# A transformer row kernel: V's channels stored by groups, V projected ahead of the scores in the first batch row, experts' biases added after the second gathering

## What is computed

```python
# attention block, on h = layernorm(layernorm(x)) with gains: 16 heads of 16 channels, each token sees 15 neighbours
q, k, v = split(h @ qkv_w + qkv_b)
attn = softmax(q . k[window] / 4);  h = (attn @ v[window]) @ proj_w + proj_b
x1 = layernorm(x) + h
x = x + x1 + gelu(layernorm(x1) @ fc1_w + fc1_b) @ fc2_w + fc2_b
# feed-forward block, on z = layernorm(x)
main = gelu(z @ W1m + b1m) @ W2m + b2m
top2 of softmax(mean(z) @ w_gate + b_gate)           # 2 of 8 experts for each batch row
expert_out = sum_k gate_k * (gelu(z @ W1e[k] + b1e[k]) @ W2e[k] + b2e[k])
out = x + a * main + (1 - a) * expert_out
```

## Time and profile before

| | |
|---|---|
| median of 3 runs | 1964.24 us |
| the profiled execution | 1966.04 us |
| its span, first to last instruction | 1964.3 us |
| TensorE's mean granted clock | 0.996 of full |
| DMA packets, under 512 B | 237054, 113564 |
| busy: VectorE, ScalarE, GpSimd | 70%, 61%, 44% of the span |

### The profile page before, as it was taken

One profiled execution on the slowest core, in us unless ns is written; L12 is line 12 of the kernel. 1 busy time (PEld: TensorE's weight loads), 2 busy tenths in 40 slices (PEclk: granted clock), 3 DMA queues, 4 the chain that ended last, 5 costly groups with the idle time before them and its releaser, 6 DMA issues.

```text
span 1964.3 us, 57553 instructions
## 1 busy us (share of the span) xinstructions
PE 1920.3 (98%) x23694; PEld 1727.4 (88%) x23694; DVE 1373.6 (70%) x2271; ACT 1191.2 (61%) x1863; POOL 854.6 (44%) x781
## 2 busy tenths in 40 slices
PE   5999999999999999999999999999999999999999
PEld 5788889898898988989888998988989889898898
DVE  6586776867768577686867768677685866768643
ACT  4575565756657566575655657566575665756554
POOL 4436245261543625335362452615336252452625
PEclk8999999999999999999999999999999999999999
DMA  4131130312204131131311303122031311313121
GB/s 118 57 82 55 38 83 28 93 55 54 72 23 98 50 81 56 33 88 39 92 55 37 84 28 92 55 60 72 28 93 44 87 51 34 87 39 93 44 60 54
DMA packets 237054, 122.41 MB, mean 62 GB/s; under 512 B 113564, under 2 KB 235768, under 8 KB 236792
## 3 DMA queue, kind: packets, MB, share of 16 engines
q1 hardware_dynamic: 234708, 117.57, 22.7%
q10 hardware_dynamic: 2084, 1.16, 0.2%
HBM read 85.52 MB, written 8.39 MB: 48 GB/s over the span
## 4 chain that ended last, share of the span: by engine, by line
PE 79%; DVE 12%; issue 4%; ACT 3%; POOL 1%; SPq 1%; DMA 0%; DVEq 0%; ACTq 0%; POOLq 0%
PE psB L233 45%; PE psA L233 27%; DVE hr_lo L533 3%; PE psA L1101 2%; PE psA L977 2%; PE psA L1064 2%; PE psA L1076 2%; DVE pr L607 2%; DVE pr L598 1%; DVE smax L605 1%; DVE acc L700 1%; DVE tm L693 1%; ACT qm L851 1%; ACT hr_hi L824 1%; DVE smax L612 1%
## 5 line engine op out<-in xcount | busy, mean ns | idle before, releaser
L533 DVE TENSOR_TENSOR hr_lo<-hf,hr_hi 128x512 fp32r<-128x512 f32 x512 | 476.6, 932 | 488.9 <-ACT hr_hi L824 487.7
L439 POOL TENSOR_SCALAR wx_hi<-raw 128x512 fp32r<-128x512 f32 x256 | 195.7, 764 | 727.2 <-DMA raw<-in_L_ffn_W2e 447.4
L824 ACT ACTIVATE hr_hi<-hf 128x512 fp32r<-128x512 f32 x512 | 323.9, 633 | 279.5 <-PE psB L233 191.2
L441 POOL TENSOR_TENSOR wx_lo<-raw,wx_hi 128x512 fp32r<-128x512 f32 x256 | 391.0, 1527 | 21.4
L233 PE MATMUL psB<-wx_hi,hr_hi 128*128 128x256 f32 x1024 | 288.5, 282 | 12.9 <-DVE acc L549 12.7
L233 PE MATMUL psB<-wx_hi,hr_lo 128*128 128x256 f32 x1024 | 286.3, 280 | 0.0
L233 PE MATMUL psB<-wx_lo,hr_hi 128*128 128x256 f32 x1024 | 285.8, 279 | 0.0
L820 ACT ACTIVATE hf<-psB,b1x 128x512 f32<-128x512 f32 x256 | 175.2, 684 | 174.1 <-PE psB L233 173.6
L233 PEld LDWEIGHTS psB<-wx_hi,hr_hi 128*128 128x128 f32 x1024 | 192.5, 188 | 28.0 <-issue 18.7
L233 PE MATMUL psB<-z_hi,wx_hi 128*128 128x512 f32 x512 | 212.0, 414 | 0.0
L233 PE MATMUL psB<-z_hi,wx_lo 128*128 128x512 f32 x512 | 202.5, 395 | 0.0
(11 more groups left out here) (151 smaller groups left out, 4772.6 us busy)
## 6 DMA issues: line engine op xcount, KB each, us to landing
raw<-in_L_ffn_W1e SPq DMA_DIRECT2D x256, 128.0 KB, 2.3
raw<-in_L_ffn_W2e SPq DMA_DIRECT2D x256, 128.0 KB, 2.2
vb<-vs SPq DMA_DIRECT2D x64, 192.0 KB
vb<-vs SPq DMA_DIRECT2D x62, 160.0 KB
out_x<-acc SPq DMA_DIRECT2D x32, 256.0 KB, 2.2
xin<-in_L_attn_x SPq DMA_DIRECT2D x15, 512.0 KB, 3.7
tm<-in_L_ffn_b2e SPq DMA_DIRECT2D x32, 128.0 KB, 3.0
raw<-in_L_attn_fc_w SPq DMA_DIRECT2D x8, 256.0 KB, 5.3
```

Source lines behind the costliest of these rows:

```text
L439: g.tensor_scalar(wx[0][:, s, :], raw[:, s, :], 1.0, 0.0, ALU.mult, ALU.add).then_inc(w_hi.sem, 1)
L441: g.tensor_tensor(wx[1][:, s, :], raw[:, s, :], wx[0][:, s, :].bitcast(f32), ALU.subtract).then_inc(w_lo.sem, 1)
L533: v.tensor_tensor(hr[1][:, c % 2, :], hf[:, c % 3, :], hr[0][:, c % 2, :].bitcast(f32), ALU.subtract).then_inc(h_lo.sem, 1)
L824: a.activation(hr[0][:, c % 2, :], hf[:, c % 3, :], ACT.Copy).then_inc(h_hi.sem, 1)
```

## The change

`vs` is stored by channel groups, [128, 2 groups, 4 tiles, 2 parities, 128 channels]. `values` on TensorE reads the weights' columns and writes PSUM in the order of the groups, and `values` on VectorE makes four operations of 128 elements a partition for two of 256. The bias of V is loaded in that order, by two DMAs. A copy to `vb` now moves 3 or 4 KB in one run per partition. Of `vb` only what no copy writes, and `attend` reads, is set to zero, with four small memsets.

In iteration 0 both halves of V are projected and evacuated before the scores (the second through bank 1 of `psB`).

The experts' biases are summed at step 11 into `b2sum`, which lies in `kT` (free between the last scores and the next keys), and added to `acc` at step 18, after the second gathering (`add_bias`). The first gathering reads `sx` and writes `acc`. `shortcut`, which overwrites `sx`, waits for the first gathering; ScalarE's `keys` wait for `acc_b`.

```diff
@@ -92,7 +92,7 @@
-        vs = sb("vs", [P, NT, 2, D])
+        vs = sb("vs", [P, G, NT, 2, KD * GW])
@@ -136,6 +136,7 @@
+        b2sum = kT[:, LEFT:LEFT + D]
@@ -184,28 +185,29 @@
-        small_in, rows_in = signal("small_in", 8, 16), signal("rows_in", 7, 16)
+        small_in, rows_in = signal("small_in", 8, 16), signal("rows_in", 8, 16)
...
+        consts, zeroed, dzero = signal("consts"), signal("zeroed", 2 * G), signal("dzero")
...
+        acc_s, acc_b = signal("acc", 6), signal("acc_b")
...
+        val, vs_s, vb_in = signal("val", 2), signal("vs", 8), signal("vb_in", 12, 16)
@@ -265,8 +267,8 @@
-                    src = vs[at:at + n, tiles[0] - back:tiles[-1] + 1 - back, :, :].rearrange("p i e (c g n) -> p i e c g n", c=KD, g=G)[:, :, :, :, gr, :]
-                    eng.dma_start(dst.rearrange("p i e c n -> p (i e c) n"), src.rearrange("p i e c n -> p (i e c) n")).then_inc(vb_in.sem, 16)
+                    src = vs[at:at + n, gr, tiles[0] - back:tiles[-1] + 1 - back, :, :]
+                    eng.dma_start(dst.rearrange("p i e c n -> p (i e c n)"), src.rearrange("p i e n -> p (i e n)")).then_inc(vb_in.sem, 16)
@@ -290,7 +292,10 @@
-            loads = [(dst[:, :], row(src).to_broadcast([P, D])) for src, dst in ((qkv_b[2 * D:3 * D], bv), (proj_b, bproj), (fc2_b, bfc2))]
+            loads = [(dst[:, :], row(src).to_broadcast([P, D])) for src, dst in ((proj_b, bproj), (fc2_b, bfc2))]
+            for g in range(G):
+                loads.append((bv[:, g * KD * GW:(g + 1) * KD * GW].rearrange("p (c n) -> p c n", c=KD),
+                              qkv_b[2 * D:3 * D].rearrange("(o c g n) -> o c g n", o=1, c=KD, g=G)[:, :, g, :].to_broadcast([P, KD, GW])))
@@ -306,7 +311,7 @@
-            sp.wait_ge(zeroed.sem, 1)
+            sp.wait_ge(zeroed.sem, zeroed.all(0))
@@ -448,12 +453,18 @@
-                    g.wait_ge(acc0.sem, acc0.at(t - 1))
+                    g.wait_ge(acc_s.sem, acc_s.at(t - 1, 1))
...
-            g.memset(vb[:, :, :, :, :, :], 0.0).then_inc(zeroed.sem, 1)
...
+            for gr in range(G):
+                first, n = GW * gr, zeroed.per // G * gr
+                g.memset(vb[first:first + LEFT, 0, 0, :, :, :], 0.0).then_inc(zeroed.sem, 1)
+                g.wait_ge(zeroed.sem, n + 1)
+                g.memset(vb[first:first + KW, HS - 1, NT - 1, :, :, :], 0.0).then_inc(zeroed.sem, 1)
+                g.wait_ge(zeroed.sem, n + 2)
@@ -490,7 +501,7 @@
-            zeros = [kT[:, 0:LEFT], kT[:, LEFT + T:ZW], pr[:, 1, :, :, KW:].rearrange("p b g k -> p (b g) k"), vs[:, :, :, :].rearrange("p i e n -> p (i e n)")]
+            zeros = [kT[:, 0:LEFT], kT[:, LEFT + T:ZW], pr[:, 1, :, :, KW:].rearrange("p b g k -> p (b g) k"), vs[:, :, :, :, :].rearrange("p g i e n -> p (g i e n)")]
@@ -541,12 +552,16 @@
                         v.wait_ge(gate_s.sem, gate_s.all(f))
-                    if part:
-                        v.wait_ge(acc_s.sem, acc_s.at(f, 2 * (part - 1) + h))
+                    if part == 2:
+                        v.wait_ge(acc_b.sem, acc_b.at(f))
+                    elif part:
+                        v.wait_ge(acc_s.sem, acc_s.at(f, h))
                     else:
-                        v.wait_ge(acc0.sem, acc0.at(f))
-                    sl = acc[:, 2 * h:2 * h + 2, :].rearrange("p i n -> p (i n)")
-                    v.scalar_tensor_tensor(sl, psB[:, 2 + h, :], gates[:, part - 1:part] if part else al[:, 1:2], sl, ALU.mult, ALU.add).then_inc(acc_s.sem, 1)
+                        v.wait_ge(x2.sem, x2.at(f, h))
+                        if f:
+                            v.wait_ge(store.sem, store.at(f - 1, h))
+                    sl, old = (a[:, 2 * h:2 * h + 2, :].rearrange("p i n -> p (i n)") for a in (acc, acc if part else sx))
+                    v.scalar_tensor_tensor(sl, psB[:, 2 + h, :], gates[:, part - 1:part] if part else al[:, 1:2], old, ALU.mult, ALU.add).then_inc(acc_s.sem, 1)
@@ -580,11 +595,13 @@
+                bank = psA[:, 2 if n or t == 0 else 0, :] if t or n == 0 else psB[:, 1, :]
...
-                    dst, src, bias = (a.rearrange("p i (h e d) -> p i h e d", e=2, d=HD)[:, :, :, p, :] for a in (
-                        vs[:, 2 * n:2 * n + 2, p, :], psA[:, 2 if n or t == 0 else 0, :].rearrange("p (i n) -> p i n", n=D),
-                        bv[:, :].unsqueeze(1).to_broadcast([P, 2, D])))
-                    v.tensor_tensor(dst, src, bias, ALU.add).then_inc(vs_s.sem, 1)
+                    for g in range(G):
+                        dst, src, bias = (a.rearrange("p i (h e d) -> p i h e d", e=2, d=HD)[:, :, :, p, :] for a in (
+                            vs[:, g, 2 * n:2 * n + 2, p, :], bank.rearrange("p (i g n) -> p i g n", i=2, g=G)[:, :, g, :],
+                            bv[:, g * KD * GW:(g + 1) * KD * GW].unsqueeze(1).to_broadcast([P, 2, KD * GW])))
+                        v.tensor_tensor(dst, src, bias, ALU.add).then_inc(vs_s.sem, 1)
@@ -690,14 +707,16 @@
                 v.wait_ge(gate_s.sem, gate_s.all(f))
-                v.scalar_tensor_tensor(b2x[:, 0, :], b2x[:, 0, :], gates[:, 0:1], b2main[:, :], ALU.mult, ALU.add).then_inc(b2_s.sem, 1)
+                if f + 1 < ROWS:
+                    v.wait_ge(score.sem, score.all(f + 1))
+                v.scalar_tensor_tensor(b2sum, b2x[:, 0, :], gates[:, 0:1], b2main[:, :], ALU.mult, ALU.add).then_inc(b2_s.sem, 1)
                 v.wait_ge(b2_s.sem, b2_s.at(f, 0))
-                v.scalar_tensor_tensor(b2x[:, 0, :], b2x[:, 1, :], gates[:, 1:2], b2x[:, 0, :], ALU.mult, ALU.add).then_inc(b2_s.sem, 1)
+                v.scalar_tensor_tensor(b2sum, b2x[:, 1, :], gates[:, 1:2], b2sum, ALU.mult, ALU.add).then_inc(b2_s.sem, 1)
...
+            def add_bias(f):
                 v.wait_ge(b2_s.sem, b2_s.all(f))
-                v.wait_ge(x2.sem, x2.all(f))
-                if f:
-                    v.wait_ge(store.sem, store.all(f - 1))
-                v.tensor_tensor(acc[:, :, :], sx[:, :, :], b2x[:, 0, :].unsqueeze(1).to_broadcast([P, NT, D]), ALU.add).then_inc(acc0.sem, 1)
+                v.wait_ge(acc_s.sem, acc_s.at(f, 3))
+                v.tensor_tensor(acc[:, :, :], acc[:, :, :], b2sum.unsqueeze(1).to_broadcast([P, NT, D]), ALU.add).then_inc(acc_b.sem, 1)
@@ -708,6 +727,7 @@
+            values(0, 1)
@@ -735,12 +755,13 @@
                             shift(t, 0)
-                            values(t, 1)
+                            if t:
+                                values(t, 1)
...
                         shift(t, 1)
-                    elif q == 6 and f >= 0:
-                        route_bias(f)
+                    elif q == 18 and f >= 0:
+                        add_bias(f)
@@ -757,6 +778,8 @@
                         attended_low(t, 0)
+                    elif q == 11 and f >= 0:
+                        route_bias(f)
@@ -837,6 +860,8 @@
+                    if t > 1:
+                        a.wait_ge(acc_b.sem, acc_b.at(t - 2))
@@ -910,7 +935,7 @@
-                            a.wait_ge(zeroed.sem, 1)
+                            a.wait_ge(zeroed.sem, zeroed.all(0))
@@ -1032,12 +1057,12 @@
-                bank = 2 if n or t == 0 else 0
+                bank = psA[:, 2 if n or t == 0 else 0, :] if t or n == 0 else psB[:, 1, :]
...
-                        last = three(pe, psA[:, bank, j * D:(j + 1) * D], [z[:, k, to:to + P] for z in zT], [w[:, k, 2 * D:] for w in wqkv],
-                                     k == 0, k == KD - 1)
+                        last = three(pe, bank[:, j * D:(j + 1) * D].rearrange("p (g c n) -> p g c n", g=G, c=KD), [z[:, k, to:to + P] for z in zT],
+                                     [w[:, k, 2 * D:].rearrange("p (c g n) -> p g c n", c=KD, g=G) for w in wqkv], k == 0, k == KD - 1)
@@ -1045,7 +1070,7 @@
-                    pe.wait_ge(vs_s.sem, vs_s.at(t, 1))
+                    pe.wait_ge(vs_s.sem, vs_s.at(t, 3))
@@ -1153,9 +1179,7 @@
                             pe.wait_ge(z3_lo.sem, z3_lo.at(t - 1, 0))
-                        else:
-                            pe.wait_ge(vs_s.sem, vs_s.at(0, 1))
-                        values(t, 1)
+                            values(t, 1)
```

More of the change, by code:

```diff
@@ L191, in build @@
         xload, store = signal("xload", 1, 16), signal("store", 2, 16)
-        consts, zeroed, dzero = signal("consts"), signal("zeroed"), signal("dzero")
+        consts, zeroed, dzero = signal("consts"), signal("zeroed", 2 * G), signal("dzero")
         small_ps, small_t = signal("small_ps"), signal("small_t")
@@ L201, in build @@
         w_hi, w_lo = signal("w_hi", NX), signal("w_lo", NX)
-        acc_s, acc0 = signal("acc", 6), signal("acc0")
+        acc_s, acc_b = signal("acc", 6), signal("acc_b")
         nb_s = signal("nb")
@@ L213, in build @@
         qk, kT_s, qm_even, qm_odd = signal("qk", 4), signal("kT", KD), signal("qm_even", 8), signal("qm_odd", 8)
-        val, vs_s, vb_in = signal("val", 2), signal("vs", 4), signal("vb_in", 12, 16)
+        val, vs_s, vb_in = signal("val", 2), signal("vs", 8), signal("vb_in", 12, 16)
```

## The result

The changed kernel takes **1953.0 us** (median of 5 runs; 1952.5 to 1954.3). The kernel before, run beside it, takes 1964.2 (5 runs, 1961.6 to 1965.3). The ratio is 0.9945 (0.9931 to 0.9960). So it is faster, by 11 us where 26.8 were forecast, and 3 us above the upper end of the range.

The account below looks back on a forecast made before the run. TensorE, busy 98%, was taken as the bound, losing time to `acc` waits and V's copies. Gain 16.3 - 1.0 + 8.4 + 3.1 = 26.8 us from 1964.2, so median 1937.4 us, range 1932 to 1950.

Parts of the forecast that it names:

- The `acc` stall: TensorE's wait at chunk 8's down product, batch rows 1 to 15: 1.09 us each, 16.3 us won by moving the bias.
- I cost these at nothing: Waits added by the moved bias operations at q=11, q=18 and `shortcut`: no cost; at most 2.2 us a row without cover.
- The bias and the groups as one sum: Steady rows: 16.3 us gained by the bias part; groups lose 1.0 us, their faster copies worth nothing more to TensorE.
- miss `h_low` of chunk 7 altogether: Steady rows: sooner copies bring weight splits 5 to 8 us sooner, so GpSimd's `bproj` addition avoids VectorE's `h_low`.
- the stall stays: Rival: GpSimd's addition still starts at 261.6, the gathering stays late, only batch row 0 gains: 1953.7 us; chance 0.11.
- V's products and evacuations: V's projection: products still start 0.12 us apart, four evacuations take about 0.88 us; 1.0 us booked lost for the run.
- The rival with the strided operand: V's 384 products slow down on strided reads; at double time 46 us lost, 1983 us; chance of slower 0.06.
- The copies: V's window copies in batch row 0: about 0.5 us each to issue, 1.5 MB at 300 GB/s landed by 30.
- four copies no longer hold up the exponential: ACT in batch row 0: its four copies stop delaying the exponential for 5.7 us, making ACT 1.2 us earlier.
- Batch row 0: First row: `attend` starts at 32.4, 8.4 us sooner, plus 3.1 us from a clock that stays full.
- TensorE doesn't stand idle from 33.1, so the clock shouldn't fall: Batch row 0, 41 to 48 us: clock at 1.00 instead of 0.50, worth 3.1 us, bounds 0 and 6.2.

Follow-up runs that it names:

- the run with the copy in it: Changed kernel with the exponential of unit 3 replaced by a copy on ScalarE from batch row 1 on: 1947.0 us, ratio 0.9914.
- the split held: Changed kernel with GpSimd's weight split of chunk 13 held until the row's fourth normalisation (unit 3) is done: 1950.3 us, ratio 0.9934.
- The run with ten more idle products: Changed kernel with `attended_high(t, 0)` behind chunk 9's gelu, plus ten idle TensorE products around the first two attends in row 0: 1948.1 us.
- copies moved, the clock at 1.00 and products cut: Kernel with `attended_high` later, ScalarE's copies first and ten more idle products, then ten instead of sixteen idle products behind the second `attend`: 1947.8 us.
- the weight loads held: Changed kernel with SP's MLP weight loads from piece 8 on held in row 0 until the first `attend` is done: 1953.5 us, ratio 0.9952.
- the copies issued first: Changed kernel with `attended_high(t, 0)` behind chunk 9's gelu, and ScalarE's four window copies ahead of both exponentials in row 0: 1947.4 us.
- two kernels with equal pitch: Changed kernel with `attended_high(t, 0)` behind chunk 9's gelu, 1950.4 us, and changed kernel with unit 3's exponential replaced by a copy, 1947.0 us.
- the run with six products inside the first: Kernel with `attended_high` later, copies first and ten more idle products, but six idle products mid first `attend` replacing three before it: 1947.8 us.

## Why the prediction was off

**The `acc` stall: right in place and price, wrong in what follows.** It was 1.09 us a row with the hidden part, and it is gone. A row without any stall takes 118.04 us, and the run with the copy in it has a rest of 1873.9 us, 14.7 under the kernel before, where 15.3 were booked. What failed is the sentence "I cost these at nothing". I had looked at the waits that the change adds, and not at the next place in the row where TensorE meets VectorE. That place stands in the trace before the change, one chunk further on:

```profile
276.43 0.96 DVE L616 TENSOR_TENSOR pr<-pr,rinv 128x768 f32<-128x768 f32 x1
...
278.48 1.08 PE L1076 MATMUL psA<-ident,pr 128*112 128x128 f32 x8
```

The normalisation ended at 277.39 and `turn` followed at 278.48: 1.09 us of slack, in a row whose stall cost 1.46 and 0.24 us. So some 0.6 us of that row was bound to come back. Done for all 15 rows (slack 0.63 to 1.19 us), this gives about 2.5 us in seven rows; in the other eight the slack was larger than the stall. The new wait costs more: 0.47 us in each of twelve rows (118.51 less 118.04) and 1.1 in one, **6.8 us** in all, an estimate from these rows. What the slack before doesn't show is the collision: `turn`'s normalisation took 0.96 us in all 15 rows before, and 1.31 (or 1.30) in 14 of 15 after. In the fifteenth, and in two rows with the groups alone, it took 0.96, and no wait is listed; with the split held the waits went in all rows but one, and the pitch is 118.16, so that the collision is 0.35 of the 0.47. The last row's wait of 0.57 adds to it.

**The bias and the groups as one sum: right only because one was booked at nothing.** The prediction put the steady gain on the bias part and nothing on the groups in steady rows. The runs show either alone to be enough. The clause that GpSimd's addition can "miss `h_low` of chunk 7 altogether" was right, and it is the mechanism of the groups part there: `h_low` takes 0.68 us with the groups alone and 0.69 in the changed kernel, instead of 2.88. The rival "the stall stays" gave 1953.7, very near the time, but its mechanism is refuted: no wait for `acc` is left.

**V's products and evacuations: right.** The products start 0.12 us apart with the strided operand, four evacuations take 0.88 us. The rival with the strided operand is refuted, and the 1.0 us booked can't be told from nothing: 118.04 is what the prediction had left for a row.

**The copies: the rate nearly right, the issue mis-sized.** 268 GB/s at full share in a steady row, for 300 taken and 175 before. The Trainium skill ("DMA: Bandwidth & Descriptors", section "Why small descriptors are slow (HBM only)") says that SBUF to SBUF copies don't suffer from small pieces; here 268 against 175 GB/s speaks against it, and the measurement decides. But issuing took 0.86 us each on SP and 1.26 on ACT in row 0, where I had 0.5 (0.74, median, in steady rows, 0.87 before). That ACT's "four copies no longer hold up the exponential" failed: ScalarE stood 4.3 us before it, 2.2 of them after its input was there. And the twelve had not landed by 30 but at about 34.4, beside SP's weight loads. The count of runs is off too, without effect: 6016 runs become 384, not 376.

**Batch row 0: 11.5 us booked, 4.8 came.** `attend` started at 34.53 instead of 32.4, put down to ACT as forecast; that is 6.3 of the 8.4. The pause of 2.26 us behind it was not in the forecast in any form. The step "TensorE doesn't stand idle from 33.1, so the clock shouldn't fall" failed: TensorE stood idle from 33.7 to 34.5 and from 35.3 to 37.6, and the clock read 0.50 from 38 to 48, so the 3.1 us for 41 to 48 didn't come. The run with ten more idle products, where that stretch is at 1.00, has a row 0 shorter by 1.5, half of the term. With copies moved, the clock at 1.00 and products cut, VectorE's normalisations hold TensorE up, and row 0 ends at 67.21: 8.5 of the 11.5.

**The sum of the misses**: 8.4 us in the rest of the run (6.8 the new wait, 0.6 the last row, 1.05 two pauses put down to issue, of 0.32 and 0.73 us) and 6.7 in row 0.

Not settled: what decides when TensorE's instructions are fetched. The packet came 1.0 us sooner with the weight loads held (33.98 for 34.95), but also 1.5 sooner with the copies issued first, so that transfers beside it play a part is likely and not shown.

## What to carry to other kernels

When a stall is to be removed, look up, for each later place in the same period where the bottleneck engine meets another, how long the input had been there: where the stall is longer than the slack, the difference comes back. Read it in every period, and as an estimate: other engines shift too, and here, where it gives 2.5 us, 6.8 came back, mostly by a collision that wasn't there before. Two edits that cure the same stall aren't two terms. A DMA issue on a computing engine's queue is worth its time on that engine, so put it where the engine would idle anyway.

## What was not expected of the hardware

- TensorE pauses for its instructions. In a stream of 128 products of 10 ns spacing it stopped for 0.7 to 2.3 us, and the end of the pause followed a 16 KB packet on the instruction queue by 2.4 to 2.7 us in twelve traces. In the later rows such pauses (0.2 to 1.8 us, none in the kernel before, one to six in the others) made 2.9 of the 3.4 us between two kernels with equal pitch.
- A copy within SBUF takes about as long to issue in long runs as in short: 0.74 us against 0.87 (medians), when runs grew from 256 B to 3 or 4 KB. A load of the experts' weights took 0.33 or 0.38 (medians).
- With ten idle products more in front of the first two `attend`s the granted clock was at 1.00 from 41 to 48 us, where it was 0.50 without them, although the pauses for instructions stayed (2.02 and 1.23 us). Of two pauses alike, 1.51 and 1.54 us in the second `attend`, one was followed by 0.50 and the other, in the run with six products inside the first, was not.
